# A routed expert layer behind attention: routed rows scattered by token group into fixed expert regions, and 17 of its 39 tiles placed ahead of the last group's router

## What is computed

```python
h = layernorm(x) * (1 + ca) + sa                    # ca, sa, ga ... from a small modulation product
x = x + ga * attention(h)                           # 16 heads of width 8, causal, low-rank q, k, v
h = layernorm(x) * (1 + cb) + sb
logits = relu(h @ Wr1 + br1) @ Wr2 + br2            # the router, 8 experts
tg, ti = top_k(softmax(logits), 2); tg = softmax(tg / 2)
out = silu(h @ Ws1 + bs1) @ Ws2 + bs2               # the shared expert, 128 -> 512 -> 128
for e in range(8):                                  # the routed experts, the same widths
    out = out + weight_of(e, tg, ti)[:, None] * (silu(h @ We1[e] + be1[e]) @ We2[e] + be2[e])
x = x + gb * out
```

## Time and profile before

| | |
|---|---|
| time, three runs | 482.98, 483.8, 485.03 us (median 483.8) |
| span of the profiled execution | 482.4 us, from its first to its last instruction |
| mean granted TensorE clock | 0.966 of full speed |
| busy: PE, DVE, ACT, POOL | 419.0, 319.8, 268.0, 140.4 us |
| last attention product | starts at 308.2 us |
| tile loop, first row turn to last result copy | 339.1 to 462.1 us |
| HBM read, written | 20.44 MB, 7.80 MB |

### The profile page before, as it was taken

One profiled execution on the slowest core, in us unless ns is written; L12 is line 12 of the kernel. 1 busy time (PEld: TensorE's weight loads), 2 busy tenths in 40 slices (PEclk: granted clock), 3 DMA queues, 4 the chain that ended last, 5 costly groups with the idle time before them and its releaser, 6 DMA issues.

```text
span 482.4 us, 9071 instructions
## 1 busy us (share of the span) xinstructions
PE 419.0 (87%) x2974; PEld 246.1 (51%) x2974; DVE 319.8 (66%) x1143; ACT 268.0 (56%) x614; POOL 140.4 (29%) x234
## 2 busy tenths in 40 slices
PE   4689899899999999999999998998668778989870
PEld 3344333534435345345344343447568568878860
DVE  5687998888889888878878815368624333534527
ACT  3353657657677575755847676464245544443723
POOL 2170530100101102502501001020757664666420
PEclk9999999999999999999999999999979995999995
DMA  4334030250302103003000057000111110112144
GB/s 140 100 112 129 36 93 10 61 172 1 93 10 57 47 1 87 15 2 95 7 1 24 1 180 193 24 22 2 52 37 45 44 46 27 40 46 44 34 136 148
DMA packets 21307, 29.09 MB, mean 60 GB/s; under 512 B 3876, under 2 KB 15381, under 8 KB 20757
## 3 DMA queue, kind: packets, MB, share of 16 engines
q1 hardware_dynamic: 18333, 23.01, 15.8%
q0 software_dynamic: 2496, 5.12, 3.8%
q10 hardware_dynamic: 432, 0.39, 0.3%
HBM read 20.44 MB, written 7.80 MB: 59 GB/s over the span
## 4 chain that ended last, share of the span: by engine, by line
PE 69%; DVE 11%; issue 7%; ACT 5%; DMA 3%; another core or an unknown queue 2%; SPq 1%; POOL 0%; DVEq 0%; POOLq 0%; ACTq 0%
PE oacc L1546 14%; PE sc L1526 11%; PE mx L1497 10%; PE sc L1817 8%; PE oacc L1828 8%; PE sc L1531 2%; DVE masked L1121 2%; PE mx L1555 2%; ACT osb L777 2%; PE sc L1629 2%; DVE mxp L1125 2%; ACT pr L886 1%; DMA S<-q_parts 1%; PE mx L1649 1%
## 5 line engine op out<-in xcount | busy, mean ns | idle before, releaser
L768 ACT ACTIVATE pr<-sc 128x512 f32<-128x512 f32 (+1 forms) x304 | 157.1, 581 | 90.6 <-PE sc L1531 50.4
L1121 DVE CUSTOM_DVE_ANT_0 masked<-mx,later 128x128 f32<-128x128 f32 (+3 forms) x256 | 111.6, 485 | 13.1 <-PE mx L1497 12.3
L1497 PE MATMUL mx<-S 72*128 72x512 bf16 (+3 forms) x384 | 111.7, 328 | 8.9 <-DMA S<-q_parts 2.2
L1526 PE MATMUL sc<-S 75*128 75x512 bf16 (+3 forms) x384 | 110.6, 328 | 0.6 <-ACT pr L768 0.3
L1125 DVE TENSOR_REDUCE mxp<-mx 128x1 f32<-128x512 f32 x128 | 82.6, 685 | 23.9 <-PE mx L1497 23.3
L1546 PE MATMUL oacc<-pr,vb 128*32 128x512 f32 (+3 forms) x768 | 74.4, 501 | 0.0
L886 ACT ACTIVATE pr<-sc,bcur 128x128 f32<-128x128 f32 x156 | 44.4, 369 | 42.9 <-PE sc L1817 23.5
L1526 PEld LDWEIGHTS sc<-S 75*128 75x128 bf16 x384 | 35.3, 97 | 47.6 <-issue 24.1
L1497 PEld LDWEIGHTS mx<-S 72*128 72x128 bf16 x384 | 34.1, 97 | 49.4 <-DVE mxp L1121 14.8
L1828 PE MATMUL oacc<-vb,pr 128*128 128x128 f32 x312 | 46.0, 294 | 10.6 <-ACT pr L886 10.3
L1817 PE MATMUL sc<-S,vb 128*128 128x128 f32 x312 | 44.6, 289 | 10.6 <-issue 10.1
(11 more groups left out here) (247 smaller groups left out, 469.3 us busy)
## 6 DMA issues: line engine op xcount, KB each, us to landing
S<-q_parts SPq DMA_DIRECT2D x48, 96.0 KB
S<-k_parts SPq DMA_DIRECT2D x21, 192.0 KB
S<-in_we SPq DMA_DIRECT2D x1, 2048.0 KB, 9.4
S<-in_we SPq DMA_DIRECT2D x4, 512.0 KB, 10.1
parts<-token_results SPq DMA_DIRECT2D x4, 512.0 KB, 5.3
x_sb<-in_x SPq DMA_DIRECT2D x4, 256.0 KB, 4.1
hidden_rows<-parts SPq DMA_DIRECT2D x4, 256.0 KB, 2.4
out_y<-attn SPq DMA_DIRECT2D x4, 256.0 KB, 2.3
```

The lines of the kernel that those rows point to most:

```text
L768: act.activation(pr[:, group % NBUF, h:h + n, at:at + w], src, ACT.Exp, scale=float(DK) ** -0.5).then_inc(s["exp_done"], 1)
L1121: ins = dve.tensor_tensor_reduce(masked[:, d % 2, w * m:w * m + w], mx[:, a % RING, w * m:w * m + w], later[:, HALF - w:HALF], 1.0, LOWEST ...
L1497: ins = pe.matmul(dst[:, w * m:w * m + w], S3[0:CROSS, r3, 1, q:q + P], S3[0:CROSS, r3, 0, kk:kk + w], start=(m == 0), stop=True, skip_gro ...
L1526: ins = pe.matmul(dst[:, w * m:w * m + w], S3[0:CROSS + 3, r3, 0, kk:kk + P], S3[0:CROSS + 3, r3, 1, q:q + w], start=(m == 0), stop=True, ...
```

## The change

It replaces the one sort at the end by four small ones, one a token group.

- Each expert gets a fixed region of 2048 slots in an HBM table `slot_rows`, rows of 129 words: 128 of the token's modulated row and one with the index where its result goes. After a group's router a unit `pf` (6 small products) and `slots_of` on DVE give each row its slot behind those that earlier groups filled, and POOL scatters the group's rows there (`send`, 8 indirect transfers a group, one for each tile and each of its two experts). Groups 0 and 1 send during tasks 5 and 6, one transfer every second score.
- Before that the whole table must hold blank rows: POOL clears a buffer at score (2, 24), and ACT's queue issues 9 transfers (`fill_slots`), one every fifth score from score (2, 34) on: 8 of 1.06 MB, each from 16 partitions of SBUF, repeated 8 times, in pieces of 8256 bytes, and one of 0.53 MB from 128 partitions. `hidden_rows` of group 0 waits for all nine, since it writes over the blank buffer.
- The 39 tiles come in three lists of 9, 8 and 22 (`tile_list` on DVE, 13 to 16 small operations): 9 tiles of rows from groups 0 and 1, 8 with group 2's, the rest after group 3's. A tile is now 128 consecutive rows of a region, so SP loads it (`load_rows`: it reads the row number into a register and issues a plain transfer, 12 buffers). POOL has only the scatters of results.
- Order after attention: one shared up product, `pf` of group 2, the last group's halves, then the tile loop. The rest of the last group's chain sits inside the loop (`CHAIN`: `at` at iteration 0, `wo` 1, `x2t` 4, `rt` 5, `lg` 6, `pf` 8), as do 15 shared up products (iterations 0 to 14) and all 16 shared down pieces (iterations 16 to 31). These units alternate between two PSUM banks.
- In the loop ACT does `x_copy`, and DVE takes the result out of PSUM with the expert's output bias added (`y_out`). The bias products, their gate turns and the one-hot matrices are gone; the shared bias is folded into `x` on POOL. The first products that kept PE busy in gaps of the last group's chain (`fill_late`) are gone.

```diff
 LATE = {...
+        (5, 0): ("pf", 0, 0),
+        (6, 0): ("pf", 1, 0),
...
+TILES = [9, 8, 22]
+FIRST_TILE = [0, 9, 17]
+FIRST_DOWN = 16
+CHAIN = {0: ("at",), 1: ("wo",), 4: ("x2t",), 5: ("rt",), 6: ("lg",)}
+BLANK_AT, FILL_AT, FILL_EVERY, FILLS = (2, 24), 34 + 2 * 38, 5, 9
+SEND_LAG, SEND_EVERY = 3, 2
...
-    order += [(kind, 3, h) for kind in ("half", "at", "wo", "x2t", "rt", "lg") for h in range(2)]
+    order += [UPS[0], ("pf", 2, 0), ("half", 3, 0), ("half", 3, 1), ("begin", 0, 0)]
+    for i in range(ROUTED):
+        order.append(("head", i, 0))
+        order += [(kind, 3, h) for kind in CHAIN.get(i, ()) for h in range(2)]
+        if i == 8:
+            order.append(("pf", 3, 0))
+        if i + 1 < len(UPS):
+            order.append(UPS[i + 1])
+        if 0 <= i - FIRST_DOWN < len(DOWNS):
+            order.append(DOWNS[i - FIRST_DOWN])
+        if i == ROUTED - 4:
+            order.append(("odds", 0, 0))
+        order.append(("tail", i, 0))
...
-            store_rows(2)
-            store_rows(3)
+            def load_rows(i):
+                phase = max(p for p in range(3) if FIRST_TILE[p] <= i)
+                if i == FIRST_TILE[phase]:
+                    sp.wait_ge(s["list_ready"], phase + 1)
+                    for g in range((0, 2, 3)[phase], phase + 2):
+                        sp.wait_ge(sent[g], 16 * 8)
+                if i >= XR:
+                    sp.wait_ge(y_stored[(i - XR) % ROWS], 16 * ((i - XR) // ROWS + 1))
+                at = sp.value_load(tile_r[0:1, i:i + 1], min_val=0, max_val=P * (NE * REGION + 7))
+                sp.dma_start(xrow[:, i % XR, :], xd[bass.ds(at, P), :]).then_inc(rows_in[i % XR], 16)
...
             def hidden_rows(g):
...
+                if g < 2:
+                    pool.wait_ge(s["filled"], 16 * FILLS)
+                else:
+                    pool.wait_ge(sent[g - 2], 16 * 8)
...
+            def send(g, n, k):
+                if n == 0 and k == 0:
+                    pool.wait_ge(s["rowi_ready"], g + 1)
+                    pool.wait_ge(s["h2_ready"], g + 1)
+                pool.indirect_dma_start(xd, bass.IndirectOffsetOnAxis(ap=rowi[:, g, k, n:n + 1], axis=0),
+                                        rowsk[:, g % 2, n, k, :], None).then_inc(sent[g], 16)
...
-            def gather(i):
...
+            def fill_slots(m):
+                act.wait_ge(s["blank_ready"], 1)
+                if m < NE:
+                    dst = xd[SLOTS * m:SLOTS * m + SLOTS, :].rearrange("(j u r) c -> u j (r c)", u=16, r=16)
+                    src = blank[16 * m:16 * m + 16, 0:16, :].rearrange("p r c -> p (r c)")
+                    act.dma_start(dst, src.unsqueeze(1).broadcast_to([16, 8, 16 * ROWW])).then_inc(s["filled"], 16)
...
+            def slots_of(g, a):
+                chained(dve.tensor_tensor(place, pfx[:, 0:4, :], carry..., ALU.add))
+                dve.tensor_tensor(carry[:, :], carry[:, :], pfx[:, 4, :], ALU.add).then_inc(s["aux_free"], 1)
+                chained(dve.tensor_tensor(place1, place..., sel[:, g], ALU.mult))
+                chained(dve.tensor_reduce(place..., place1, AX_X, ALU.add))
+                dve.tensor_copy(rowi[:, g], place...).then_inc(s["rowi_ready"], 1)
...
+            def y_out(i):
+                dve.wait_ge(s["dn_ready"], i + 1)
+                if i >= ROWS:
+                    dve.wait_ge(y_stored[i % ROWS], 16 * (i // ROWS))
+                dve.tensor_tensor(yst[:, i % ROWS:i % ROWS + 1, :], oacc[:, i % 2:i % 2 + 1, 0:P],
+                                  be2_sb[:, bass.ds(experts[i], 1), :], ALU.add).then_inc(s["y_done"], 1)
```

More of the change, by code:

```diff
@@ L160, in adaln_layer @@
     ORDER = attention_order(T)
-    AUX = [x for x in ORDER if x[0] not in ("score", "weigh", "xturn")]
+    AUX = [x for x in ORDER if x[0] not in ("score", "weigh", "xturn", "begin", "head", "tail", "odds")
+           and (x[0] != "down" or x[2] == 3)]
+    HELD, PRIOR, LAST_TURN = unit_banks(AUX)
     PLACE = {x: a for a, x in enumerate(AUX)}
@@ L168, in adaln_layer @@
     NLOAD = 9
[L169 to L171 removed]
     TOK = B * S
[L173 removed]
+    SLOTS = S * B
+    REGION = SLOTS // P
+    ROWW = C + 1
+    XR = 12
     ROWS = 8
     ROUND = 1.5 * 2 ** 23
[L176 to L179 removed]
     FREE = 8
[L181 removed]
     with ExitStack() as ctx:
@@ L195, in adaln_layer @@
         bank = [sc[:, 0, :], sc[:, 1, :], sc[:, 2, :], mx[:, 0, :]]
+        unit = [(mx[:, 0, :], mx[:, 1, :], mx[:, 2, :], sc[:, 2, :])[b] for b in HELD]
         x_sb = sb("x_sb", [P, NT, C], F32)
@@ L1165, in _ @@
             bests = []
-            for a, (kind, t, k) in enumerate(AUX):
+            listed = []
+            experts = []
+            for kind, t, k in ORDER:
+                a = PLACE.get((kind, t, k))
                 if (kind, t, k) in ON_ACT:
@@ L1224, in _ @@
                         best_index(t, 1)
+                        choose(t)
+                elif kind == "pf":
+                    slots_of(t, a)
+                    if t == 1:
+                        listed.append((0, 0))
+                    elif t > 1:
+                        for part in range(4):
+                            tile_list(t - 1, part)
                 elif kind == "half":
                     half_out(k, a)
-                else:
+                elif kind == "out":
                     attn_out(t, k, a)
-            chained(dve.tensor_copy(topf[:, :, :], topi[:, :, 0:2]))
@@ L1319, in _ @@
-            dve.scalar_tensor_tensor(out=goal[:, :], in0=slot[:, :], scalar=-1.0, in1=unused[:, :],
-                                     op0=ALU.add, op1=ALU.add).then_inc(s["goal_ready"], 1)
+                elif kind == "begin":
+                    for i in range(2):
+                        experts.append(expert(i))
+                        up_copy(i)
+                    down_copy(0)
+                elif kind == "head":
+                    if t + 2 < ROUTED:
+                        experts.append(expert(t + 2))
+                        up_copy(t + 2)
+                    if t + 1 < ROUTED:
+                        down_copy(t + 1)
+                elif kind == "down" and k == 3:
+                    shared_out(t, a)
+                elif kind == "odds":
+                    gate_sums()
+                elif kind == "tail":
+                    y_out(t)
@@ L1631, in up @@
-            def up(c, fs):
-                for f in fs:
-                    if c >= 1:
-                        pe.wait_ge(s["silu_done"], NF * (c - 1) + f + 1)
-                    up_part(c, f, up_bank[f]).then_inc(s["up_ready"], 1)
-            def down_main(c, i, dst):
+            def up(c, f, a):
+                if c == 0 and f == 0:
+                    pe.wait_ge(s["exp_done"], NU * T)
+                if f == 0:
+                    for h in range(2 if c == 3 else 1):
+                        pe.wait_ge(*freed(("x2t", c, h)))
+                ring_free(a)
+                pe.matmul(unit[a], sh_up[:, P * f:P * f + P], h2T[:, 512 * c:512 * c + 512], start=True,
+                          stop=True).then_inc(s["aux_ready"], 1)
@@ L1681, in fill @@
                     pe.matmul(dst, identb[:, :], parts[:, 0, 0, 0:HALF], start=True, stop=True)
-            def fill_late(n):
-                for _ in range(n):
-                    pe.matmul(sc[:, 2, 0:P], identb[:, :], identb[:, :], start=True, stop=True)
             pe.wait_ge(s["mod_done"], 1)
@@ L1852, in _ @@
-            for i in range(4):
-                down_piece(3, i)
+                elif kind == "pf":
+                    prefix(t, a)
+                elif kind == "up":
+                    up(t, k, a)
+                elif kind == "down":
+                    down(t, k)
+                elif kind == "begin":
+                    turn_rows(0)
+                    turn_rows(1)
+                    up_tile(0)
+                elif kind == "head":
+                    if t + 2 < ROUTED:
+                        turn_rows(t + 2)
+                    if t + 1 < ROUTED:
+                        up_tile(t + 1)
+                elif kind == "tail":
+                    down_tile(t)
+                elif kind == "out":
+                    turn_out(t, k, a)
```

769 lines of the change are left out of this document (315 added, 454 removed).

## The result

The changed kernel takes 516.9 us (four runs, 512.82 to 519.07), the one before 483.4; the ratio is 1.069, interval 1.063 to 1.076. The forecast was 470, the range 457 to 492. The profiled execution has a span of 513.9 us, 31.5 more than before's 482.4.

A forecast was written before the change was run, and what follows sets the result against it. PE has most work from the last attention product on but idles 21.8 of 121 us, with late signals and reduced clock. Tail -19.1 and attention +6 give net -13.1 from 483.8: 470.7, predicted 470, range 457 to 492.

The forecast's parts named there:

- the fills: Blank-row fills in attention: 11.3 MB with loads at 254 GB/s would end at 190, before 197.69; cost 0.
- Rival C: Fills come late at 122 GB/s, `hidden_rows(0)` waits, PE stands 10 to 29 us: 490 us; chance 0.28.
- slower: Forecast direction: time above 486.2 us, chance 0.26, of which 0.19 from Rival C and 0.07 from Rival D.
- my estimate by the page: By the skill's port rule, eight fills take 81 us one after another, ending near 227; not in the sum.
- Attention beside the fills: Added DVE blocks 3 us, `pf` twice 1.0, waits from sends and issues 2: together +6, between 1 and 10.
- late signals: ACT and DVE start long after PE's product ended; 4 us taken in the tail, between 0 and 21.8.
- Rival D: Late signals belong to POOL's indirect transfers as such, 0.39 us each, 27 against 8.5 summed: 489 us; chance 0.10.
- The tail: Last attention product to last result copy: 13.5 start, 103.4 PE work, 15.5 waits; 132.4 after 151.5, so -19.1.
- start chain: Between last attention product and first down product: 13.5 us, between 10 and 17.
- tile 17's rows: Last group's sent rows load by 372, tile 17 is turned at 375; fits by 3 us, no wait.
- the end stage: Behind the last result copy, 20.3 us to the span's end, not touched by the change.
- Iterations: Tile loop: 2.75 us each with a shared product, to number 30, and 1.9 behind.

The follow-up runs named there:

- changed_again: The changed kernel run again, unchanged: 518.36 us, 1.069 of the kernel before.
- fills_small: The changed kernel with its 8 fills cut from 2048 slots each to the 128 where each region's last row falls for this input: 485.69 us.
- ends_paced_again: ends_and_paced run once more, unchanged, on a chip without late signals: 467.28 us, 1.021 of the kernel before.
- ends_and_paced: Changed kernel without region fills (blanks written behind region ends), sends of groups 0 and 1 each waiting for a score unit: 467.25 us, 1.015 of before, quicker chip.
- before_bursts: The kernel before plus 24 indirect writes nobody waits for, in three back-to-back blocks of eight on POOL in attention: 511.4 us, 1.054 of before.
- small_sends_paced: fills_small with each send of groups 0 and 1 waiting on POOL for its score unit, one every third: 476.74 us, 0.986 of before.

## Why the prediction was wrong

**The step that failed** is the fills: "I take no cost, as the loads leave half of the engines idle". The rate at share 0.48 was scaled up to 254 GB/s. But the share counts time, and transfers out of 16 neighbouring partitions filled that time with 102 to 127 GB/s from 155 to 165. Their cost was 31.8 us by the landmarks (32.9 in changed_again) and 31.2 by the time of fills_small, instead of 0. Rival C had the rate, at 122 GB/s, and a chance of 0.28, but the wrong place: it priced only `hidden_rows(0)` and counted the loads of queries and keys as part of the stream, when it is these that PE needs next. PE paid for the backlog from 160 us on, at the first load due in it, not at 216. So the high end of the range, 492, was short by 25. On the direction: slower had 0.26.

The Trainium skill's "SBUF — State Buffer", section "Door 1: The DMA port swizzle", was quoted in the prediction against my own row, about 104 GB/s for 16 neighbouring partitions. With that figure the trace agrees over the first 15 us, at 97 to 127 GB/s, loads included. Later stretches reach 273 (probably since fills from different partitions then lie beside each other; no run separates this), so my estimate by the page, 81 us for eight in a row, was too long: the share falls to 0.29 by 205 to 210. It was the better guide to the sum than my scaled row.

**Attention beside the fills**: summed +6, range to +10. It was 11.9 in the first profile, 17.3 in changed_again and 9 to 19 in the variants with small fills or none. Paced sends bring it to 6.3 (125.4 against 119.1), and on chips without late signals it is 7 to 10 (126.0 and 127.4 in ends_paced_again and ends_and_paced, 117.5 and 119.1 in the two runs of before with single writes). So the term was about right for the added work, inside its range, and lacked the late signals of the sends in attention; I had put those at 4 us, in the tail alone. Rival D named the mechanism. Its price of 0.39 us a transfer assumed that every one costs the same; the paced run speaks for blocks, but single writes were never run on a chip with late signals.

**The tail**: 132.4 summed, 136.2 measured, so -15.3 for -19.1. The first down product came 16.4 us behind the last attention product, not 13.5, with waits of 1.85, 3.91 and 2.29 us in the start chain; 16.4 is inside the bounds given. PE did not wait for tile 17's rows, as forecast, and the end stage's 20.3 us are 20.6. Iterations last 2.79 us (turns at 440.96 and 443.75), for 2.75, and 1.90 behind number 30.

**Why the tail gained at all** was argued half right. On chips without late signals the tail part of before is 126.2 us and that of the new order 126.6 to 128.0. To the end of the span it is 150.9 against 148.2 to 149.5: putting 17 tiles ahead of the router bought 1 to 3 us there, less than attention pays for it. On the other kind the tail part is 24.7 us longer in before, with a gather and a scatter for each tile, and 8 to 11 longer in the new order; the 15 us are the difference. My sum had this as 30.1 us of losses turning into 8.5, which is more than the whole of its -19.1; it did not ask what would be left without them.

**What stays open.** Why some chips have late signals and others not. How much of before_bursts is POOL's queue. How much of the 9.0 us of small_sends_paced is the pacing: it is not shown on one chip with fills_small. Whether ends_and_paced beats before on a chip with late signals (by parts 476, not run there).

No kernel tried beats before on both kinds of chip. small_sends_paced is 1.4% faster on one kind and was not run on the other; it is fitted to this input.

## What to carry to other kernels

A DMA share of 0.5 doesn't mean that half the rate is free: price a new bulk transfer by the partitions that it comes from, and look first at which small loads share the DMA engines with it and when each is due. Sends or scatters "every n steps" need a wait on the step; a place in the queue of an engine that waits for nothing makes blocks. And when a sum consists mostly of losses that vanish, ask what it gives on a chip that never had them.

## What the runs showed of the hardware that was not expected

Chips differ by 5% on the same kernel (459.7 and 483.5 us). Up to the last attention product they are within 1.7 us of each other; the difference is in the tail, where POOL issues indirect transfers back to back and where on one kind ACT and DVE are released together 1 to 5 us after PE's recorded end. On that kind 24 indirect writes that nobody waits for cost 27 to 29 us in blocks of eight, and 24 plain ones 5 (3.8 on the other kind). Single ones, four scores apart, cost nothing (-0.4 and +1.5 us) on the other kind, the only one where they were run. And fills in two halves, from partitions that lie apart, moved 174 to 214 GB/s at about half the DMA share (0.52 to 0.56) at which those from 16 neighbouring partitions moved 102 to 127.
